# The halo copies and the first tap of v ahead of Z plus identity of level 6, on VectorE of a gated delta-rule kernel

## What is computed

```python
q, k, v = (silu(short_conv(x @ W, taps)) for W in (Wq, Wk, Wv))   # causal, four taps, per channel
q, k = l2norm(q) * SCALE, l2norm(k)
def step(S, inp):                      # for each token, S is [128, 128] per head
    qt, kt, vt, gt, bt = inp
    S = S * exp(gt)[..., None]
    err = einsum('bhk,bhkv->bhv', kt, S)
    delta = bt[..., None] * (vt - err)
    S = S + kt[..., None] * delta[:, :, None, :]
    return S, einsum('bhk,bhkv->bhv', qt, S)
x = x + attention(layernorm(x)); x = x + moe(layernorm(x))
```

## Time and profile before

| | |
|---|---|
| median of 3 runs | 5455.79 us (5451.93 to 5457.29) |
| the profiled execution | 5453.22 us |
| its span | 5451.3 us |
| PE busy | 5158.7 us, 95% |
| VectorE busy | 4336.8 us, 80% |
| ScalarE, POOL busy | 59%, 41% |
| granted clock of TensorE from 238 to 4560 us | 1.00 |

### The profile page before, as it was taken

One profiled execution on the slowest core, in us unless ns is written; L12 is line 12 of the kernel. 1 busy time (PEld: TensorE's weight loads), 2 busy tenths in 40 slices (PEclk: granted clock), 3 DMA queues, 4 the chain that ended last, 5 costly groups with the idle time before them and its releaser, 6 DMA issues. The chain is left out here.

```text
span 5451.3 us, 87981 instructions
## 1 busy us (share of the span) xinstructions
PE 5158.7 (95%) x27204; PEld 3574.5 (66%) x27204; DVE 4336.8 (80%) x8284; ACT 3224.4 (59%) x6602; POOL 2245.1 (41%) x3689
## 2 busy tenths in 40 slices
PE   5599999999999999999999999999999996999999
PEld 2277777777777777777777777777777775444444
DVE  6699999999999999999999999999999995121110
ACT  3377777777777777777777777777777775010110
POOL 2154545455545454545454555454555453000000
PEclk8799999999999999999999999999999998999999
DMA  2111111111111111111111111111111111322121
GB/s 81 44 31 40 34 39 33 40 32 40 34 40 32 39 32 40 32 40 32 40 32 40 32 40 32 40 32 40 32 40 32 32 32 37 106 99 85 54 70 52
DMA packets 192052, 235.73 MB, mean 43 GB/s; under 512 B 41576, under 2 KB 136424, under 8 KB 187504
## 3 DMA queue, kind: packets, MB, share of 16 engines
q1 hardware_dynamic: 111016, 188.22, 11.5%
q10 hardware_dynamic: 80584, 41.95, 2.6%
HBM read 183.75 MB, written 46.38 MB: 42 GB/s over the span
## 5 line engine op out<-in xcount | busy, mean ns | idle before, releaser
L744 PE MATMUL bank<-xT,weights 128*128 128x512 f32 x4096 | 2087.3, 607 | 33.4 <-PEq L159 33.4
L763 PE MATMUL bank<-KQ,KR 128*128 128x128 f32 x7168 | 999.7, 282 | 87.5 <-DVE KQ L1074 85.9
L1059 DVE SCALAR_TENSOR_TENSOR conv<-pre,taps,conv 128x512 f32<-128x512 f32 x1152 | 985.0, 855 | 22.2 <-ACT conv L1276 8.1
L1510 POOL TENSOR_TENSOR KR<-KR,decay_u 128x256 f32<-128x256 f32 x768 | 672.2, 875 | 714.9 <-PE bank L763 714.3
L763 PEld LDWEIGHTS bank<-KQ,KR 128*128 128x128 f32 x7168 | 877.6, 191 | 109.5 <-DVE KQ L1074 107.4
L1074 DVE TENSOR_TENSOR KQ<-KQ,decay_u 128x512 f32<-128x512 f32 x896 | 906.1, 1011 | 29.0 <-PE bank L763 4.0
L744 PEld LDWEIGHTS bank<-xT,weights 128*128 128x128 f32 x4096 | 673.8, 191 | 247.7 <-issue 226.4
L1089 DVE COPY_PREDICATED all_pairs<-level_mask,bank 128x512 f32<-128x512 int32 x896 | 795.3, 888 | 0.0
L1363 ACT ACTIVATE X<-bank 128x256 fp32r<-128x256 f32 x768 | 297.8, 388 | 433.9 <-PE bank L821 433.4
L1119 DVE TENSOR_TENSOR ZI<-bank,ident_each 128x256 fp32r<-128x256 f32 x768 | 322.4, 420 | 244.1 <-PE bank L795 228.0
L1558 POOL CAST XX<-X 128x128 fp32r<-128x128 f32 x640 | 249.2, 389 | 645.9 <-ACT X L1363 628.3
(11 more groups left out here) (197 smaller groups left out, 9470.1 us busy)
## 6 DMA issues: line engine op xcount, KB each, us to landing
decay_u<-decay_scratch SPq DMA_DIRECT2D x128, 510.0 KB
beta_u<-beta_scratch SPq DMA_DIRECT2D x128, 256.0 KB
y_in<-y_scratch SPq DMA_DIRECT2D x32, 1024.0 KB, 4.8
y_scratch<-y_rn ACTq DMA_DIRECT2D x112, 256.0 KB, 2.3
xt<-in_L_attn_hidden_states SPq DMA_DIRECT2D x8, 1024.0 KB, 5.5
x_in<-in_L_attn_hidden_states SPq DMA_DIRECT2D x28, 256.0 KB, 5.0
out<-o_out ACTq DMA_DIRECT2D x28, 256.0 KB, 2.0
w<-in_L_ffn_W SPq DMA_DIRECT2D x8, 704.0 KB, 4.9
```

Source lines behind the costliest of these rows:

```text
L744: last = nc.tensor.matmul(bank[w % 2][:], weights[par][:, w, k, :], xT[:, k, u % J * UC:(u % J + 1) * UC], start=k == 0, stop=k == KC - 1)
L763: last = nc.tensor.matmul(to[:, :, i], KR[:, cols(i)], halves(KQ[m % 2][:, :, cols(i)], l, 1), start=True, stop=True)
L1059: nc.vector.scalar_tensor_tensor(conv[:, w], taps_from(w, t), taps[par][:, w, t:t + 1], conv[:, w], ALU.mult, ALU.add).then_inc(steps.sem, 1)
L1510: nc.gpsimd.tensor_tensor(firsts, firsts, second.to_broadcast([P, 2, UC >> (l + 2), 1 << l]), ALU.mult).then_inc(keys_scaled.sem, 1)
```

## The change

In each step, VectorE's list has `add_identity_to_z(6)` three calls later: behind `last_query()`, the halo of unit z and the first tap of v, and directly ahead of `scale(5)`. The instructions, their number, their operands and the semaphores are the same, as are the lists of all other engines.

```diff
             add_identity_to_z(5)
             scale(4)
             keep_pairs(4)
-            add_identity_to_z(6)
             last_query()
             halo(z, s.z_first, a, qk_conv_steps, 2 * (TAPS - 1), (0, 1), qk_halo_ready)
             convolve(2, (1,))
+            add_identity_to_z(6)
             scale(5)
             convolve(2, (2,))
             keep_pairs(5)
```

## The result

| | before | after |
|---|---|---|
| median of 4 runs | 5454.31 us (5451.93 to 5457.29) | 5418.78 us (5414.3 to 5424.36) |
| ratio | | 0.9936, 95% interval 0.992 to 0.9951 |
| profiled execution, its span | 5453.22, 5451.3 us | 5415.82, 5414.0 us |
| mean granted clock of TensorE over the span | 0.983 | 0.978 |

The kernel became faster by 0.64%, 35.5 us between the medians and 37.4 us between the profiled executions. The forecast was 5414. The time is near it, but two errors of about 20 and 25 us, of opposite sign, stand behind that.

A forecast was written before the change was run, and what follows sets the result against it. Bound: VectorE from level 6 on, then PE to the next Z. 6 × (−0.60) + 0.44 + 0.52 = −2.64 us per head, −42 us over 16 heads, gave 5411, plus 2.6 to the median: 5414 us; range 5375 to 5458.

The forecast's parts named there:

- What bounds the kernel: Attention loop: VectorE from level 6 on, then PE to the next Z; at most 1.16 us gained per ordinary unit.
- Both stalls: PE waits for late VectorE at level(6), 0.88 us, and at refine(c, 1), 0.28 us, per ordinary unit; both go.
- The turns with POOL: In VectorE's gap, copies wait for first_x, the tap ends 0.55 us behind add_squares; identity 0.50 us late in ordinary units.
- three kinds of unit: Per head of 8 units: 6 ordinary, 1 first chunk, 1 where a is the last chunk; identity 0.50, 1.40, 2.25 us late.
- Step 4: PE's inverse_x(6) waits for the identity with no slack taken: +0.56 us per ordinary unit, bounds 0.36 and 1.2.
- first chunk: One unit in 8, a head's first: identity late costs +1.46 us, stalls of 1.02 us go, net +0.44 us.
- last-chunk step: One unit in 8, with last_query: identity late costs 2.31 us, stalls of 1.51 and 0.28 us go, net +0.52 us.
- lost overlap: A late start costs PE its overlap with the load of weights: 0.06 us added to each delay.
- rival 1: POOL gets between the copies and again ahead of the tap; identity 1.10 us late, +36 us, 5492 us; chance 0.14.
- Rival 3: Copies and tap get ahead of POOL, before first_x; identity in time, −130 us, 5326 us; chance 0.11.
- Rival 2: ScalarE holds VectorE, too late for refine(c, 1); 36 us not gained, 5450 us, no change; chance 0.13.
- The slower side: The whole kernel gets slower, through rival 1 and the worst of Rival 2; chance 0.15.

The follow-up runs named there:

- experiment 1: Against the changed kernel, last_query and the two copies go behind the identity, so only the tap of v stays ahead of it; 5330.27 us.
- experiment 5: Against the changed kernel, POOL's add_squares (L1530) adds only 4 of its 512 columns, leaving out the rest of that sum; 5309.64 us.
- experiment 2: Against the changed kernel, the tap of v goes behind the identity, with last_query and the two copies still ahead of it; 5382.58 us.
- experiment 4: Against the changed kernel, the new order is kept only in the last-chunk step, with the identity first in all others; 5481.59 us.
- experiment 3: Against the changed kernel, the identity comes first again in the last-chunk step only and stays moved in all others; 5391.93 us.

## Why the prediction came out as it did

1. **What bounds the kernel:** right. Both stalls went together (0.86 and 0.28 us a unit), and when the identity was in time too (experiment 1) an ordinary unit fell from 33.86 to 32.79 us, 1.07 of the 1.16 that the prediction named as the limit.
2. **The turns with POOL:** right. The tap ended 0.55 us behind L1530; the identity was late by 0.52, 1.40 and 2.25 us in the three kinds of unit, for 0.50, 1.40 and 2.25 forecast. The Trainium skill (SBUF — State Buffer, Who interferes with whom) has the rule of the shared port pair, which spoke against the change; by experiment 5 the rule is what cost 0.38 us a unit, and by experiments 1 and 2 its price depends on which instruction gets the first turn.
3. **Step 4, no slack at L821:** wrong in size. The prediction took 0.56 us and 0.36 as the bound with 0.2 of slack; 0.38 was measured. The same 0.2 is missing in the first chunk (1.25 for 1.46) and in the last-chunk step (2.11 for 2.31). Of the 0.2 us, 0.14 is slack, as the identity's own delays show, and 0.06 is the lost overlap that the sum added here, though no row showed it for L821. The prediction read "just in time" from a record of PE that starts as soon as its releaser ends, with no idle time printed; that does not say that PE had nothing left to do. Per head the sum had 6 × 0.18 + 0.21 + 0.20 = 1.5 us too much at L821, 24 us in all, and some 4 us too much gain at the other stalls.
4. **First chunk:** forecast +0.44, measured by waits 1.25 − 0.17 − 0.61 = +0.47. **Last-chunk step:** forecast +0.52, measured +0.2.
5. **What was not foreseen:** the half-clock stretches, 16 × 1.56 = 25 us lost. No term and no rival had them. The profile before could not show them, as PE's longest wait there was 1.5 us; but the sum wrote down a new wait of 2.3 us, the longest in the attention, and priced it at its length alone.
6. **The rivals:** rival 1 (copies apart) fell for this change: in all of the 110 units with copies they passed together, also where 11 had not before. It is no empty rival, as the 57 of 110 in experiment 4 show. Rival 3 fell: VectorE still met `first_x`. Rival 2 fell for this change too. Its stall came in experiment 2, though not by way of ScalarE. The slower side came true only for a part, the last-chunk step alone (+0.43%), mostly by a mechanism that none of the rivals named.

The net: 62 us by waits, 42 forecast; less 25 us of clock; 37 measured. The mechanism at the port was foreseen rightly, but that the forecast of 5414 us came within 5 us of 5418.78 is luck, since the two errors nearly cancel.

## What to carry to other kernels

When instructions move into an engine's idle gap ahead of a critical one, ask which of them gets the first turn at a shared port: here the one 512-column tap in the first turn gained 2.3%, two tiny copies ahead of it left 0.6%. Look at the rare steps apart from the common ones: the change made in the one step in eight that carried extra work, and nowhere else, gave a kernel slower by 0.43%, most of it from that step. And price a new wait of the matrix engine that is longer than all it has now above its length, since the clock may fall behind it.

## What the hardware showed that was not expected

**The clock fell behind waits of 1 to 2 us.** Half-clock stretches of 3.4 us, each costing 1.56 us, stood behind waits of 2.1 us at L821 (11 of 15 in the change, 14 of 15 in experiment 4) and of 1.25 us in first chunks (5 of 15, and 4 of 15 in experiment 3), with PE busy in 97% and more of the attention. None stood behind the 1.5 us waits at L763 in the kernel before, nor behind 1.45 us at L821 in the last-chunk steps of experiment 2. So the length of the wait is not all that decides, and what else does stays open; no run here was made to find it.

The Trainium skill (TensorE: Matmul & The Clock Gate, What's actually happening) says that the gate follows how busy PE has been recently. The runs agree that it is the recent past that counts, not the mean over the stage: experiment 4 had the stretches with PE as busy as before.

**Two tiny copies wait for a whole instruction of POOL, and may be parted.** They move 16 columns each. In the changed kernel they wait for the end of POOL's running instruction and then both pass before its next, in 110 of 110 units. Elsewhere the second one is sometimes held by itself: in 11 of 110 before, in 57 in experiment 4 and in 17 in experiment 1. Before and in experiment 4 it is close: in ordinary units the first copy took 0.28 to 0.31 us where the second passed, and 0.30 to 0.33 where it was held. What shifts the balance stays open.
